# Six-sublayer decoder on one core: ternary feed-forward in one pass with its weights on chip, weight check moved into two attention stages

## What is computed

```python
def _L1_ffn_ref(x, w1_w, w1_s, w2_w, w2_s, h1_w, h1_s, h2_w, h2_s, w3_w, w3_s):
    def _tlin(x, w, s):
        return jnp.einsum('bsi,oi->bso', x, w) * s
    h = jax.nn.silu(_tlin(x, w1_w, w1_s)) * _tlin(x, w2_w, w2_s)
    h = jax.nn.gelu(_tlin(h, h1_w, h1_s), approximate=False)
    h = jax.nn.gelu(_tlin(h, h2_w, h2_s), approximate=False)
    return _tlin(h, w3_w, w3_s)
...
x = _layernorm(x + _L1_ffn_ref(x, ...), axis=-1)
```

## Time and profile before

| | us |
|---|---|
| times of the kernel before, median (lowest to highest) | 2274.41 (2271.41 to 2274.49) |
| profiled execution, its own time | 2266.7 |
| span of the program in it | 2264.9 |
| latent attention, slots | 88 to 434 |
| cross attention, slots | 488 to 834 |
| quantised feed-forward | 851 to 1044 |
| state space | 1044 to 1320 |
| full attention | 1320 to 1499 |
| ternary feed-forward and output | 1499 to 2265 |
| PE busy over the span | 1829.9 (81%) |
| DVE, ACT busy | 1247.3 (55%), 1035.4 (46%) |

### The profile page before, as it was taken

One profiled execution on the slowest core, in us unless ns is written; L12 is line 12 of the kernel. 1 busy time (PEld: TensorE's weight loads), 2 busy tenths in 40 slices (PEclk: granted clock), 3 DMA queues, 4 the chain that ended last, 5 costly groups with the idle time before them and its releaser, 6 DMA issues. The chain is left out here.

```text
span 2264.9 us, 34711 instructions
## 1 busy us (share of the span) xinstructions
PE 1829.9 (81%) x12518; PEld 1506.4 (67%) x12518; DVE 1247.3 (55%) x2577; ACT 1035.4 (46%) x1914; POOL 328.1 (14%) x506
## 2 busy tenths in 40 slices
PE   2799999769999985873667658838999996699996
PEld 1677777557888863552666648837887885588885
DVE  3566666446666646883677758862332222354553
ACT  1366766425555555553454435553443344422220
POOL 4443432010111103451000000000000000000000
PEclk9799999879999997996787879978999998799998
DMA  5775656067667611000000011131111113221212
GB/s 140 163 137 107 128 118 128 14 150 153 135 139 138 130 27 56 0 0 27 0 0 0 0 56 57 52 112 52 60 46 60 60 56 121 68 75 44 68 56 75
DMA packets 121121, 170.31 MB, mean 75 GB/s; under 512 B 14912, under 2 KB 88896, under 8 KB 117824
## 3 DMA queue, kind: packets, MB, share of 16 engines
q1 hardware_dynamic: 115888, 164.63, 29.1%
q10 hardware_dynamic: 5120, 4.20, 1.1%
HBM read 101.68 MB, written 55.05 MB: 69 GB/s over the span
## 5 line engine op out<-in xcount | busy, mean ns | idle before, releaser
L57 PE MATMUL ps<-ffn_b_gT_hi,ffn_b_h_hi 128*128 128x512 f32 x512 | 202.1, 395 | 9.5 <-DVE ffn_b_gT_lo L2077 9.5
L57 PE MATMUL ps<-ffn_a_hT_hi,ffn_a_h_hi 128*128 128x512 f32 x512 | 204.1, 399 | 2.5 <-ACT ffn_a_result L1936 2.5
L57 PE MATMUL ps<-ffn_b_gT_lo,ffn_b_h_hi 128*128 128x512 f32 x512 | 201.7, 394 | 0.0
L57 PE MATMUL ps<-ffn_a_hT_lo,ffn_a_h_hi 128*128 128x512 f32 x512 | 201.6, 394 | 0.0
L654 ACT ACTIVATE cross_probs<-ps 128x512 f32<-128x512 f32 x192 | 115.5, 603 | 132.3 <-PE ps L464 81.4
L654 ACT ACTIVATE latent_probs<-ps 128x512 f32<-128x512 f32 x192 | 115.5, 603 | 105.2 <-PE ps L464 55.4
L217 POOL TENSOR_TENSOR shifted<-moments,eps 128x4 f32<-128x4 f32 x24 | 5.3, 223 | 1091.6 <-DVE moments L188 1091.6
L858 DVE TENSOR_REDUCE latent_neg_max<-ps 128x2 f32<-128x512 f32 (+1 forms) x192 | 129.6, 681 | 48.4 <-PE ps L443 31.6
L858 DVE TENSOR_REDUCE cross_neg_max<-ps 128x2 f32<-128x512 f32 (+1 forms) x192 | 130.1, 682 | 17.1 <-PE ps L443 17.0
L1936 ACT ACTIVATE ffn_a_result<-ps,ffn_a_sh 128x512 f32<-128x512 f32 x64 | 43.2, 687 | 182.8 <-PE ps L57 182.8
L443 PE MATMUL ps<-keys,queries 96*128 96x512 f32 x256 | 124.0, 485 | 0.0
(11 more groups left out here) (415 smaller groups left out, 5486.0 us busy)
## 6 DMA issues: line engine op xcount, KB each, us to landing
ffn_between<-ffn_a_result SPq DMA_DIRECT2D x64, 256.0 KB, 2.0
ffn_b_fresh<-ffn_between SPq DMA_DIRECT2D x64, 256.0 KB, 3.2
latent_split<-latent_qk_hi SPq DMA_DIRECT2D x16, 512.0 KB, 3.6
latent_split<-latent_qk_lo SPq DMA_DIRECT2D x16, 512.0 KB, 4.5
queries<-latent_split SPq DMA_DIRECT2D x32, 256.0 KB, 4.9
keys<-latent_split SPq DMA_DIRECT2D x32, 256.0 KB, 6.7
cross_split<-cross_qk_hi SPq DMA_DIRECT2D x16, 512.0 KB, 3.0
cross_split<-cross_qk_lo SPq DMA_DIRECT2D x16, 512.0 KB, 4.1
```

The lines of the kernel that those rows point to most:

```text
L57: last = nc.tensor.matmul(out, l, r, start=start and n == 0, stop=stop and n == len(passes) - 1, **kw)
```

## The change

It does four things.

- **The feed-forward runs in one pass over 16 states** (256 rows at a time instead of 512). All weights stay on chip, without `lo` halves. For each state: `gate_and_up`, `hidden_layer` with `h1`, `hidden_layer` with `h2`, and the `w3` products, with the work of neighbouring states in between: round j does `h2` of state j, `h1` of state j+1, the transpose of state j+2, `w3` of state j, gate and up of state j+2. Nothing goes through `ffn_between`. Each state's output is stored when it is normalised.
- **The weights are no longer split at the head of each part.** They are copied within DRAM (`to_stage`, 11 MB, issued by SP in the quantised feed-forward), `w1`, `w2`, `h1` are loaded during full attention (`core.early`, two loads of 512 KB in each of six steps), `h2` and `w3` at the start of the feed-forward (`late`).
- **The check whether they are exact is made in 44 pieces of 128 by 512**, 16 in the latent attention (one for each slot) and 28 in the cross attention (two for each of 14 slots): a load (SP), a rounding copy (`round_piece`, ACT), a comparison with a count (`compare_piece`, DVE). At the start of the feed-forward PE sums the counts and chooses the program.
- The mask's float32 form uses another tile's space, and the loop of SP in full attention is unrolled.

```diff
+                def load_piece(u):
...
+                    if u >= 2:
+                        sp.wait_ge(piece_compared, u - 1)
+                    sp.dma_start(raw_piece[:, u % 2], core.pieces[BASE + u]).then_inc(piece_in[u % 2], 16)
...
+                def round_piece(u):
...
+                    act.wait_ge(piece_in[u % 2], 16 * (u // 2) + 16)
+                    if u >= 1:
+                        act.wait_ge(piece_compared, u)
+                    nc.scalar.copy(rounded[:], raw_piece[:, u % 2]).then_inc(piece_rounded, 1)
...
                     if live(s):
+                        round_piece(piece_of(s, 0))
                         exponentials(s, 1, "B")
...
                     if live(s):
+                        round_piece(piece_of(s, 1))
                         exponentials(s, 2, "B")
...
+                    dve.wait_ge(piece_rounded, u + 1)
+                    raw = raw_piece[:, u % 2]
+                    nc.vector.scalar_tensor_tensor(raw, raw, 1.0, f32(rounded[:]), ALU.mult, ALU.not_equal, accum_out=core.differing[:, BASE + u:BASE + u + 1]).then_inc(piece_compared, 1)
...
+                for dst, src in core.to_stage:
+                    sp.dma_start(dst, src).then_inc(core.weights_staged, 16)
...
-                with sp.Fori(1, STEPS) as j:
+                sp.wait_ge(core.weights_staged, 16 * len(core.to_stage))
+                for j in range(1, STEPS):
                     sp.wait_ge(xT_raw, CHAINS * j)
                     sp.wait_ge(cT_ready, CHAINS * j)
                     load_pair(j)
+                    for u in range(2 * j - 2, min(2 * j, len(core.early))):
+                        sp.dma_start(f32(core.early[u][0]), core.early[u][1]).then_inc(core.early_in, 16)
...
-def feed_forward(nc, core, w):
+def feed_forward(nc, core, w, out):
...
+                load_state(0)
+                for dst, src in ((s1, "w1_s"), (s2, "w2_s"), (sh1, "h1_s"), (sh2, "h2_s")):
                     sp.dma_start(dst[:], w[src]).then_inc(scales_in, 16)
+                for u, (dst, src) in enumerate(late):
+                    sp.dma_start(f32(dst), src).then_inc(late_in[u], 16)
+                sp.dma_start(s3[:], w["w3_s"].partition_broadcast(P)).then_inc(scales_in, 16)
+                sp.wait_ge(x_turned, 1)
+                load_state(1)
...
+                def gate_and_up(general, i):
+                    pe.wait_ge(xT_ready, i + 1)
+                    for p in range(PAIR):
+                        for tile, base, done, freed, level in ((w1, GATE_BANK, gate_raw, gated, PAIR * i + p - 1), (w2, UP_BANK, up_raw, u_ready, PAIR * i + p - 1)):
+                            if p >= 2:
+                                pe.wait_ge(freed, level)
+                            for a in range(2):
+                                m = 2 * p + a
+                                for c in range(DT):
+                                    last = two_parts(general, halved(base + p % 2)[:, a, :], tile[:, c, m * P:(m + 1) * P], halves(xT, ALL, c), 1, c == 0, c == DT - 1, skip_group_check=True)
+                            last.then_inc(done, 1)
...
+                def program(general):
+                    gate_and_up(general, 0)
+                    pe.wait_ge(pair_split, PAIR)
...
+                    hidden_layer(general, h1, uT, wait_free)
+                    turn_state(1)
+                    gate_and_up(general, 1)
+                    for u in range(len(late)):
+                        pe.wait_ge(late_in[u], 16)
+                    rounds(general)
...
+                    def steps(j, more, more_state):
+                        pe.wait_ge(pair_split, 12 * j + 8)
+                        hidden_layer(general, h2, gT, lambda p: pe.wait_ge(activated, 8 * j + 3 + p))
+                        if more:
+                            pe.wait_ge(pair_split, 12 * j + 12)
+                            hidden_layer(general, h1, uT, lambda p: pe.wait_ge(activated, 8 * j + 7 + p))
+                        if more_state:
+                            turn_state(j + 2)
+                        pe.wait_ge(y_taken, j + 1)
+                        for c in range(IT):
+                            if c % 2 == 0:
+                                pe.wait_ge(pair_split, second_pair(j, c // 2, more) + 1)
+                            for t in range(TT):
+                                last = two_parts(general, halved(Y_BANK)[:, t, :], halves(hT, ALL, c, slice(t * P, (t + 1) * P)), w3[:, c, :], 0, c == 0 and t == 0, c == IT - 1, skip_group_check=True)
+                        last.then_inc(down_raw, 1)
+                        if more_state:
+                            gate_and_up(general, j + 2)
...
+                split_state(0)
+                act.wait_ge(scales_in, 80)
+                gate_pairs(0)
+                for p in range(PAIR):
+                    hidden_pair(p, p + 1, sh1, 3 + p)
+                split_state(1)
+                gate_pairs(1)
...
-                for b in range(B):
-                    sp.dma_start(out[b].rearrange("(t p) d -> p t d", p=P), core.X[:, b, :].rearrange("p (t d) -> p t d", d=D)).then_inc(out_done, 16)
-                sp.wait_ge(out_done, 16 * B)
```

More of the change, by code:

```diff
@@ L422, in _ @@
                         load_context(s + 4)
+                    for n in range(3):
+                        if piece_of(s, n) is not None and piece_of(s, n) + 2 < COUNT:
+                            load_piece(piece_of(s, n) + 2)
             @block.tensor
@@ L1837, in feed_forward @@
-        s1, s2, sh = (sb(n, [P, IT]) for n in ("s1", "s2", "sh"))
-        lo_used = sb("lo_used", [1, 1], mybir.dt.int32)
-        split_weights(nc, core, "ffn_aw", [(w["w1_w"], *w1), (w["w2_w"], *w2), (w["h1_w"], *h1)], lo_used)
-        x_in = sb("x_in", [P, CT, D])
-        xT = pair("xT", [P, DT, CH])
-        gate, hidden = sb("gate", [P, 2, CH]), sb("hidden", [P, 2, CH])
-        hT = pair("hT", [P, IT, CH])
-        result = sb("result", [P, 2, CH])
-        scales_in, x_copied, x_turned, xT_hi, xT_ready = sem("scales_in"), sem("x_copied"), sem("x_turned"), sem("xT_hi"), sem("xT_ready")
@@ new lines, in feed_forward @@
+        s3 = sb("s3", [P, D])
+        xT, uT, gT, hT = pair("xT", [P, DT, S]), pair("uT", [P, IT, S]), pair("gT", [P, IT, S]), pair("hT", [P, IT, S])
+        slots = sb("slots", [P, 2, 2, S])
+        x_in, gate = core.x_plus[:, TT:2 * TT], core.x_now
+        y_scaled, rows = core.x_plus[:, 0:TT], core.rows
+        late = [(h2[:, 2 * n:2 * n + 2, :], core.staged["h2_w"][:, 2 * n:2 * n + 2, :]) for n in range(IT // 2)] + [(w3[:], core.staged["w3_w"])]
+        ones, inexact = sb("ones", [P, 1]), sb("inexact", [1, 1], mybir.dt.int32)
@@ new lines, in feed_forward @@
+        count = sb("count", [1, 1])
+        late_in = [sem(f"late_in{u}") for u in range(len(late))]
+        scales_in, ones_ready, counted, judged = (sem(n) for n in ("scales_in", "ones_ready", "counted", "judged"))
+        x_copied, x_turned, xT_hi, xT_ready = (sem(n) for n in ("x_copied", "x_turned", "xT_hi", "xT_ready"))
+        gate_raw, up_raw, gated, u_ready, u_hi = (sem(n) for n in ("gate_raw", "up_raw", "gated", "u_ready", "u_hi"))
+        hidden_raw, activated, pair_split = (sem(n) for n in ("hidden_raw", "activated", "pair_split"))
@@ L1852, in feed_forward, with second_pair @@
+        def second_pair(j, p, more):
+            return 12 * j + 12 + p if more else 12 * (B - 1) + 8 + p
         with nc.Block() as block:
@@ L1912, in _, with two_parts @@
-                transpose_chunk(0)
-                if_lo_used(nc, pe, lo_used, program)
+                def two_parts(general, out_ap, left, right, split, start, stop, **kw):
+                    for n in range(2):
+                        a, b = (left[n], right) if split == 0 else (left, right[n])
+                        if general:
+                            a, b = f32(a), f32(b)
+                        last = nc.tensor.matmul(out_ap, a, b, start=start and n == 0, stop=stop and n == 1, **kw)
+                    return last
@@ new lines, in split_state, with gate_pair @@
+                def split_state(i):
+                    act.wait_ge(x_turned, i + 1)
+                    nc.scalar.copy(xT[0][:], halved(XT_BANK)).then_inc(xT_hi, 1)
+                def gate_pair(i, p):
+                    act.wait_ge(gate_raw, PAIR * i + p + 1)
+                    if p >= 2:
+                        act.wait_ge(u_ready, PAIR * i + p - 1)
+                    for a in range(2):
+                        last = nc.scalar.activation(gate[:, 2 * (p % 2) + a], halved(GATE_BANK + p % 2)[:, a, :], ACT.Silu, scale=s1[:, 2 * p + a:2 * p + a + 1])
+                    last.then_inc(gated, 1)
@@ new lines, in u_pair_hi, with hidden_pair @@
+                def u_pair_hi(i, p):
+                    act.wait_ge(u_ready, PAIR * i + p + 1)
+                    nc.scalar.copy(uT[0][:, 2 * p:2 * p + 2], slots[:, p % 2]).then_inc(u_hi, 1)
+                def hidden_pair(p, raw, scales, free):
```

(17 more changed lines are left out.)

403 lines of the change are left out of this document (173 added, 230 removed).

## The result

The changed kernel took 2219.82 us (median of four runs, 2216.70 to 2220.97), the kernel before beside it 2272.91 (2265.80 to 2274.49): a ratio of 0.977, with a 95% interval of 0.9746 to 0.9794. So the change gains 53 to 57 us. I forecast 76, that is 2198 us, with a range of 2182 to 2232: the sign and the range hold, and the time is 22 us above the forecast.

The account below looks back on a forecast made before the run. PE was taken as the bound, with about 100 of the feed-forward's 765.6 us product-free. Single-pass feed-forward -79.2, attention +2.8, other edits +0.4 gave -76 from 2274.4: 2198 us, range 2182 to 2232.

Parts of the forecast that it names:

- attention 2.8: Cross attention: checking pieces make DVE some 0.2 us late in each of 14 slots, 2.8 us; latent attention nothing.
- other edits 0.4: Copies inside DRAM, early loads, the mask's place and the unrolled loop: hidden or free, 0.4 us for all.
- Step 1: Feed-forward head: fifth scale, landing at 1519.0 behind 5 MB, holds ACT's first Silu; PE pauses, goes on at 1519.9.
- rival F: Feed-forward head: fifth scale lands early between the big loads, so no pause; -9 us, 2189, chance 0.05.
- Steps 2 and 3: Head after the pause: 32 products, partly at lower clock, 6.0 us; waits 2.5 and 3.1, `h1` 14.7, gate and up 7.4.
- Step 4: Feed-forward rounds 0 to 13: 0.115 us a product, no exposed wait, 40.9 us each, 572.6 in all.
- Step 5: Last feed-forward rounds: `h2`, `h1`, `w3` 33.1 us, then `h2`, `w3` 18.4, to 2177.7.
- The tail: After the last products: one state's scaling, addition and layer norm 5 us, store 2.2, issue and end 0.8.
- Rival A: Feed-forward products run at the cross attention's pace, 0.120 us: +26 us, 2224, chance 0.14.
- Rivals B, C and D: Too short a cover in rounds, +21 us, 0.10; attention pieces fully exposed, +56, 0.05; PE's clock falling in rounds, +217, 0.04.
- Rival E: Feed-forward: weight loads add to the products, 0.303 us each: +963 us, 3161, chance 0.02.

Follow-up runs that it names:

- e10: The changed kernel, unaltered, measured again on another chip: 2214.19 us, 0.9749 of the kernel before.
- e3: Changed kernel without the loads, rounding copies and comparisons of the 44 pieces, counts set to zero: 2212.38 us, 0.9754 of before.
- e2: Changed kernel with the feed-forward's fifth scale loaded ahead of the 5 MB of late weights: 2206.65 us, 0.9729 of before.
- e11: Changed kernel with the fifth scale first, weights and `hT` at 160 modulo 256, streamed operands and `w3` at 16: 2179.44 us, 0.9604 of before.
- e1: Changed kernel with 33 series of 48 products behind its end, operands at chosen places; 256 columns took 0.1133 to 0.1200 us a product.
- e6: Changed kernel with another 49 series behind its end, at other places, distances and widths; one series at distance 64 ran at 0.1133 and later 0.1178 us.
- e8: Changed kernel with 54 series behind its end, eleven places four times each, some on multiples of 64 bytes; aligned at distance 64: 0.1133 us four times.
- e5: Changed kernel with two unused tiles that bring all feed-forward operands to distance 64 modulo 256: 2201.29 us, 0.970 of before.

## Why the prediction was right, and where it was 22 us off

Against its own profiled execution I forecast 2190.7, and it took 2220.97: 30.3 us more. The median is only 22 above its forecast, as this profile had the long stages named above. By the steps:

- **Ahead of the feed-forward**, +3.2 forecast (attention 2.8, other edits 0.4), +8.6 measured (SP's first load at 1507.91 for 1499.31). The last cross slot starts 2.4 us later; the rest is in stages that scatter: in e10 the same program ends full attention some 8 us earlier and has a span of 2210.4. The 2.8 for the pieces doesn't show: e3 gains nothing by leaving them out.
- **Step 1**, right. PE goes on 21.3 us behind the first load; I had 20.6, with ACT's first Silu released by the scale. A wait that I didn't see lies under it: PE starts its products only at 1517.51, after 6.15 us of idle time at its entry into the chosen program. The split of state 0 ends at 1512.71, so for the last 4.8 of these nothing that the profile shows held it. As the late scale holds the Silus longer, this costs nothing here; that step 1 came out right though it left this wait out is luck. e2, where the scale is early, gained 10.4 us in its trace, of which 7.6 are the scale's; rival F had 9.
- **Steps 2 and 3**, too short by 4.2 (4.9 for the whole head). Right for the first restart (6.3 us for 32 products, I had 6.0), and for the waits (2.7 and 2.9, I had 2.5 and 3.1). What failed in them is that the clock falls once: it fell again behind waits of 2.41 and 2.33 us, and `h1` took 16.8 instead of 14.7, gate and up 9.2 instead of 7.4. Of these 3.9 us some 3.2 are the lower clock, the rest the pace of step 4.
- **Step 4**, the term that was mis-sized. The structure is right: no wait, PE at 1.00, rounds equal to 0.05 us. But 0.115 was part B's pace at part B's place; here it is 0.1187. 14 rounds took 590.9 us, not 572.6: +18.3. I had also read the old pace from part B alone. Part A has 1536 of the 2560 products of 512 columns and took 0.2333 for each (125 steps from 1571.5 to 1600.8), that is 0.117 for half the width; 0.115 was the pace of the better part only. **Step 5** the same, 53.2 for 51.5. The tail came out at 7.9 for 8.0.
- Rival A, with 0.14, was the case that happened, though not for the reason I gave: for rounded float32, no stage or kind of operand has a pace, its place has. I chose 0.115 "as weights and operands are of part B's kind"; the kind doesn't matter, and when the place was set right (e11) the pace was 0.1133, the lower bound that I had kept, and the time of the whole 2179 (0.9604), below my forecast with the help of e2. That the range held is owed to its upper bound, which stood at rival A's 0.120 a product.
- Rivals B, C and D fall to the unbroken PE rows, e3, and the clock of 1.00 in the rounds.
- Rival E falls. A weight load has a record of 0.188 to 0.189 us here too, with products 0.1187 apart, so loads overlap each other and the products. The Trainium skill (TensorE: Matmul & The Clock Gate, The mechanism) lets a load overlap products in flight only when it is for another row group; the trace disagrees again. The same section also lets a load for the background weight buffer go ahead of products in flight, which would fit the trace; no run here shows which buffer a load uses.
- The Trainium skill (TensorE: Matmul & The Clock Gate, Wait — 56ns, not 53.3ns?) gives a distance of N / 2.4 GHz plus some 2.5 ns for products at full clock, an estimate of 0.109 for 256 columns. No series of rounded float32 got there: 0.1133 to 0.1200, by the place. The bf16 products of the quantised feed-forward do, with starts 0.109 apart for 256 columns and 0.216 for 512 at full clock in the changed kernel's profile. For rounded float32 the measurement decides.

## What to carry over

When a change moves or resizes tiles, the rate of a PE-bound loop can shift by up to 6% with nothing waiting: measure the distance of starts at the new place, and give the sum a range for it. Short series after the kernel's end, one for each place, map this in a single run, but a place must be tried in the whole kernel, since the pace can change from round to round. And where one wait needs several small loads, put all of them in front of the big ones.

## What the runs showed of the hardware that I had not expected

- The addresses of weights and streamed operand within a partition set the pace of back-to-back products: 0.1133 to 0.1200 us for 256 columns of rounded float32, 0.2267 to 0.2335 for 512, with the distance modulo 256 bytes (e1, e6, e8). At 384 columns the two distances tried, 128 and 64, gave 0.176 and 0.177. At 128 columns both gave 0.112, hardly less than 256 columns at the best place, so halving the width once more would nearly double the time for the same work. Each product has its own weight load in all series; whether that load sets the 0.112 was not tested.
- At one and the same place two paces are open, 0.1133 and 0.1178 at distance 64, 0.1186 and 0.1200 at 128; a series keeps its pace to its end, and a kernel can change it from round to round (e5, e6, e8). What picks it stays open; the place of e11 showed only the fast one, in five series, in the gate, up, `h1` and `h2` products of all rounds of its profile, and in five executions within 7 us.
- PE fell to the lower level (0.213 us for 256 columns) behind idle times of 2.41 and 2.33 us in the head, while the rounds, with no idle time, stayed at 2.4 GHz throughout. It is no sure thing: the same two waits stand in all twelve profiles of the new feed-forward, and the clock fell behind 17 of the 24.
- At its entry into a chosen program PE stood for 6.15 us (4.85 in e2), of which 4.8 with its operands ready (3.5 in e2; 3.5 to 6.3 in the twelve profiles). What holds it there stays open.
